# A mixture-of-experts stage on one Trainium2 core: the experts' up weights loaded once into SBUF, and copied slot by slot by ScalarE

## The reference

```python
x = x + attention(_ln_c(x), ...)              # 12 heads, 7x7 neighbourhood, 16 registers
t = _to_tokens(x)
t = t + ffn(_ln_t(t), ...)

# ffn: T = 4608 tokens, 16 experts, top 2, inner width 512; shared expert 1024 wide
scores = jax.nn.softmax(xf @ gate_w.T, axis=-1)
topw, topi = jax.lax.top_k(scores, TOP_K)
comb = jnp.zeros((T, N_EXPERTS), xf.dtype).at[jnp.arange(T)[:, None], topi].set(topw)
h = jax.nn.silu(jnp.einsum('td,eid->tei', xf, w1)) * jnp.einsum('td,eid->tei', xf, w3)
h = h * comb[:, :, None]
y = jnp.einsum('tei,edi->td', h, w2)
z = jax.nn.silu(xf @ sw1.T) * (xf @ sw3.T) @ sw2.T
return (y + z).reshape(Bb, Ss, D)
```

## Time and profile before

| | |
|---|---|
| median of 3 runs | 1109.38 us (1109.3 to 1111.13) |
| profiled execution, its own time | 1112.27 us |
| its span (first to last instruction) | 1110.5 us |
| granted TensorE clock, mean | 0.987 |
| PE busy | 1053.0 us (95%) |
| PEld, DVE, ACT, POOL busy | 855.9, 489.1, 437.7, 486.1 us |
| moved by DMA | 164.39 MB, of which 87 x 768 KB are up weights |

### The profile page before, as it was taken

How to read it: one execution, slowest core, us unless ns; L and a number is a source line. 1 busy time by engine, 2 the same in 40 slices (tenths; PEclk the granted TensorE clock), 3 DMA queues, 4 the chain that set the end, 5 groups by cost and what they waited for, 6 DMA issues and landing times. The chain is left out here.

```text
span 1110.5 us, 32641 instructions
## 1 busy us (share of the span) xinstructions
PE 1053.0 (95%) x12184; PEld 855.9 (77%) x12184; DVE 489.1 (44%) x1826; ACT 437.7 (39%) x974; POOL 486.1 (44%) x746
## 2 busy tenths in 40 slices
PE   6897999999999999899999999999999999999991
PEld 4564777777777766566776777999999999999990
DVE  4664888888888736622222222222222222222220
ACT  2776888888888721111111111222222222222210
POOL 2111556565656400266663000555555555455541
PEclk9998999999999999999999999999999999999996
DMA  4554344444444421023223225888888888788855
GB/s 116 184 196 128 99 133 135 131 138 132 135 134 133 129 57 39 21 60 96 65 66 101 72 69 191 218 221 223 222 223 222 220 222 224 219 224 224 225 132 142
DMA packets 110703, 164.39 MB, mean 148 GB/s; under 512 B 14576, under 2 KB 83848, under 8 KB 110360
## 3 DMA queue, kind: packets, MB, share of 16 engines
q1 hardware_dynamic: 90232, 141.97, 39.6%
q0 software_dynamic: 19056, 20.14, 12.0%
q10 hardware_dynamic: 1264, 0.22, 0.1%
HBM read 130.42 MB, written 35.34 MB: 149 GB/s over the span
## 5 line engine op out<-in xcount | busy, mean ns | idle before, releaser
L627 POOL DMA_INDIRECT acc_dram<-ys,lists x87 | 137.6, 1581 | 255.1 <-DVE ys L1093 152.2
L1086 DVE TENSOR_TENSOR m_h<-m_sg,ps 128x512 f32<-128x512 f32 x87 | 59.8, 688 | 287.2 <-ACT m_sg L748 184.9
L705 ACT ACTIVATE probs<-probs,nmax 128x212 f32<-128x212 f32 x432 | 168.4, 466 | 4.6 <-DVE nmax L858 4.6
L1398 PE MATMUL ps<-xa,w13r 128*128 128x128 f32 x1392 | 169.7, 275 | 0.3 <-ACT xa L742 0.3
L1398 PEld LDWEIGHTS ps<-xa,w13r 128*128 128x128 f32 x1392 | 162.3, 192 | 0.5 <-issue 0.5
L1303 PE MATMUL ps<-c_x,sw13a_sb 64*128 64x384 f32 x768 | 145.6, 489 | 6.3 <-DVE s_h L1041 4.5
L858 DVE CUSTOM_DVE_ANT_0 probs<-ps,bmask 128x212 f32<-128x212 f32 x432 | 134.8, 368 | 24.0 <-PE ps L1209 23.8
L735 ACT ACTIVATE s_sg<-ps 128x384 f32<-128x384 f32 x96 | 47.0, 490 | 240.4 <-PE ps L1303 172.4
L748 ACT ACTIVATE m_sg<-ps 128x512 f32<-128x512 f32 x87 | 51.9, 597 | 219.4 <-PE ps L1403 196.9
L1414 PE MATMUL ps<-w_sb,m_h 128*128 x696 | 136.4, 339 | 0.0
L1223 PE MATMUL ps<-ident_sb,probs 128*98 128x128 f32 x864 | 119.0, 280 | 0.2
(11 more groups left out here) (140 smaller groups left out, 1283.4 us busy)
## 6 DMA issues: line engine op xcount, KB each, us to landing
w13r<-in_w13a SPq DMA_DIRECT2D x87, 512.0 KB
w13r<-in_w13b SPq DMA_DIRECT2D x87, 256.0 KB
vst<-v_dram SPq DMA_DIRECT2D x144, 147.0 KB
v_dram<-a_v SPq DMA_DIRECT2D x12, 576.0 KB, 3.1
w_sb<-in_w SPq DMA_DIRECT2D x8, 768.0 KB
xn_dram<-xn SPq DMA_DIRECT2D x36, 128.0 KB
a_x<-in_x SPq DMA_DIRECT2D x12, 288.0 KB, 3.5
x_p<-in_x SPq DMA_DIRECT2D x36, 96.0 KB
```

Source lines behind the costliest of these rows:

```text
L627: nc.gpsimd.indirect_dma_start(acc_dram, bass.IndirectOffsetOnAxis(ap=lists[:, j, 0:1], axis=0), ys[:, j % V8, :], None, compute_op=ALU.ad ...
L705: nc.scalar.activation(here, here, ACT.Exp, bias=nmax[:, batch % 2, r:r + 1], scale=-1.0).then_inc(b_exp, 1)
L1398: mm(ps[:, g + k, 128 * f:128 * (f + 1)], w13r[:, j % RING, k, 128 * f:128 * (f + 1)], xa[:, j % 2, 0:128], start=f == 0, stop=False, skip ...
```

## The change

The ring of four that SP fills from DRAM is taken away. In its place `w13_sb` holds the up weights of all 16 experts (96 KB per partition). SP loads them in `c_band(0)` to `c_band(7)`, two experts at a time in two transfers (1024 KB and 512 KB), with no wait of their own. In the experts' stage ACT takes the slot's expert number into a register and copies that expert's 1536 columns into a ring of two, `wring`. The copy for slot j waits until up(j-2) is done. ACT's order becomes xT_out(j+1), weights_out(j+1), d_silus(j); the copy for slot 0 waits for the routing, for all 32 weight transfers and for the last up product of the shared expert, whose weights lay where `wring` is. Several tiles get other places in SBUF, among them `s_h`, `s_sg`, `c_x2`, `xg`, `xa` and `w2_sb`; `w13_sb` covers the attention's keys and queries. SP has nothing left to issue between the shared expert and the output.

```diff
-        w13r = place("w13r", [128, RING, 3, INTER], f32, at)
+        w13_sb = place("w13_sb", [128, EX, 3, INTER], f32, at)
...
+        at = [b_end]
+        wring = place("wring", [128, 2, 3, INTER], f32, at)
...
-            def load_w13(j):
-                if j >= RING:
-                    sp.wait_ge(d_a, j - RING + 1)
-                    sp.wait_ge(d_b, j - RING + 1)
-                e = sp.value_load(slot_expert[0:1, j:j + 1], min_val=0, max_val=EX - 1)
-                sp.dma_start(w13r[:, j % RING, 0:2, :], w13a[:, ds(e, 1), :, :].squeeze(1)).then_inc(d_up[j % RING], 16)
-                sp.dma_start(w13r[:, j % RING, 2, :], w13b[:, ds(e, 1), :].squeeze(1)).then_inc(d_up[j % RING], 16)
+            def load_w13(n):
+                two = slice(2 * n, 2 * n + 2)
+                sp.dma_start(w13_sb[:, two, 0:2, :], w13a[:, two, :, :]).then_inc(d_w13, 16)
+                sp.dma_start(w13_sb[:, two, 2, :], w13b[:, two, :]).then_inc(d_w13, 16)
...
-                if n == NB - 1:
-                    for j in range(RING):
-                        load_w13(j)
+                if n < EX // 2:
+                    load_w13(n)
...
-            for j in range(RING, USED):
-                load_w13(j)
...
+            def weights_out(j):
+
+                e = act.value_load(slot_expert[0:1, j:j + 1], min_val=0, max_val=EX - 1)
+                if j >= 2:
+                    act.wait_ge(d_a, j - 1)
+                    act.wait_ge(d_b, j - 1)
+                nc.scalar.copy(wring[:, j % 2, :, :].rearrange("p k x -> p (k x)"),
+                               w13_sb[:].rearrange("p e k x -> p (e k x)")[:, ds(e * (3 * INTER), 3 * INTER)]
+                               ).then_inc(d_wA, 1)
+
+            act.wait_ge(r_done, 1)
+            act.wait_ge(d_w13, 16 * EX)
+            act.wait_ge(c_b, 8 * NB)
+            weights_out(0)
             xT_out(0)
             for j in range(USED):
                 if j + 1 < USED:
                     xT_out(j + 1)
+                    weights_out(j + 1)
                 d_silus(j)
...
-                pe.wait_ge(d_up[j % RING], 32 * (j // RING) + 32)
+                pe.wait_ge(d_wA, j + 1)
```

More of the change, by code:

```diff
@@ L46, in metaformer_block @@
     USED = (2 * T - EX) // 128 + EX
-    RING = 4
     XW = 256
@@ L150, in metaformer_block @@
         at = [arena]
-        w13r = place("w13r", [128, RING, 3, INTER], f32, at)
-        s_h = place("s_h", [128, 8, BAND], f32, at)
-        s_sg = place("s_sg", [128, 2, BAND], f32, at)
+        w13_sb = place("w13_sb", [128, EX, 3, INTER], f32, at)
+        stage = at[0]
+        w2_sb = place("w2_sb", [128, EX, 4, D], f32, at)
+        after_w2 = at[0]
         xg = place("xg", [128, V8, XW], f32, at)
         xa = place("xa", [128, 2, XW], f32, at)
[L156 to L164, removed]
+        assert qk_end <= stage and at[0] <= b_end
         at = [stage]
@@ L182, in metaformer_block @@
         assert at[0] <= after_w2
-        at = [after_w2]
-        c_x2 = place("c_x2", [128, 3, D], f32, at)
-        at = [max(b_end, at[0])]
+        at = [b_end]
         sw13a_sb = place("sw13a_sb", [128, 2, SINTER], f32, at)
@@ L189, in metaformer_block @@
         c_x = place("c_x", [128, 2, 2, BAND], f32, at)
+        s_sg = place("s_sg", [128, 2, BAND], f32, at)
+        c_x2 = place("c_x2", [128, 3, D], f32, at)
+        s_h = place("s_h", [128, 8, BAND], f32, at)
         assert at[0] <= top, at[0]
+        at = [b_end]
+        wring = place("wring", [128, 2, 3, INTER], f32, at)
+        assert at[0] == b_end + 4 * 3 * SINTER
+        at = [at[0] + 4 * 8 * D]
+        m_sg = place("m_sg", [128, 2, INTER], f32, at)
+        m_h = place("m_h", [128, 2, INTER], f32, at)
+        at = [b_end + 4 * (3 * SINTER + 8 * D + 6 * BAND + 3 * D)]
+        ys = place("ys", [128, V8, D], f32, at)
         ps = ctx.enter_context(nc.psum_tensor("ps", [128, 8, 512], f32))
@@ L285, in metaformer_block @@
         d_down = sem("d_down")
-        d_up = sems("d_up", RING)
+        d_w13 = sem("d_w13")
+        d_wA = sem("d_wA")
         d_g = sems("d_g", V8)
@@ L1397, in up @@
                     for k in range(2):
-                        mm(ps[:, g + k, 128 * f:128 * (f + 1)], w13r[:, j % RING, k, 128 * f:128 * (f + 1)],
+                        mm(ps[:, g + k, 128 * f:128 * (f + 1)], wring[:, j % 2, k, 128 * f:128 * (f + 1)],
                            xa[:, j % 2, 0:128], start=f == 0, stop=False, skip_group_check=True)
@@ L1402, in up @@
                         half = slice(64 * k, 64 * (k + 1))
-                        ins = mm(ps[:, g + k, 128 * f:128 * (f + 1)], w13r[half, j % RING, 2, 128 * f:128 * (f + 1)],
+                        ins = mm(ps[:, g + k, 128 * f:128 * (f + 1)], wring[half, j % 2, 2, 128 * f:128 * (f + 1)],
                                  xa[half, j % 2, 128:256], start=False, stop=True, skip_group_check=True)
```

## The result

The changed kernel is faster, by 0.6%. Over 8 runs each, its median is 1105.51 us (1104.32 to 1107.7) against 1112.13 us (1109.3 to 1131.92) of the kernel before, a ratio of 0.9942, 95% interval 0.992 to 0.9965. The forecast was 1107.5 us and most likely no measurable change, by a sum of -1.9 us; -6.6 us were measured between these medians. As much as the median, the spread changed: from 22.6 us between the fastest and the slowest run to 3.4. All ratios here leave out runs more than 1.5% above the fastest of their kernel, while medians and ranges count every run.

What follows compares the result with a forecast made beforehand. The prediction took PE as the bound, at 4.60 us per slot. Removing 3.4 us of backlog, all else 0, gave 1108.9 us from the profiled run or 1106.0 from the median; the middle was 1107.5, range 1105.0 to 1112.5.

Steps and rivals of the forecast that it cites:

- PE untouched: Experts' stage: PE stays at 4.60 us per slot, gaining and losing 0; with a backlog partly or wholly removed, chance 0.55.
- The copy and its place: ACT, each slot: copy 1.53 us plus register load 0.6, together 2.1, fitting the 2.50 us idle before SiLU; cost 0.
- The point from which ACT decides: Experts' stage: cover gone when copy and register load exceed 3.5 us; beyond it each 0.1 us costs 8.6 us.
- Start of the stage and early loads: First expert slots and shared bands 0 to 7: first copies ready in time, added loads fit SP's waits; cost 0.
- rival 3: Shared stage: bursts of the new loads stall PE, up to 8 x 1.84 = 14.7 us, time 1122; chance 0.09.
- the one stalled band: Shared expert: a band with seven gathers beside a down-weight load took 26.0 us against 23.70; 1.84 us lost.
- The backlog: Program's tail: POOL's chain of additions is late through slow landings; without loads the last addition starts 3.4 us earlier.
- The sum: Whole kernel: 1110.5 - 3.4 + 0 = 1107.1 us span, 1108.9 with the 1.77 us around it.
- I take the middle, 1107.5: Forecast median: between 1108.9 us (median run has hardly any backlog) and 1106.0 us (it has it too).
- 3.4 plus 0.1: Program's tail: upper bound of the backlog gain, 3.4 us plus 0.1 for each of two landings, so 3.6.
- Rival 1: Experts' stage: loads were hidden anyway, slow landings having another cause or runs no backlog; time 1109, chance 0.25.
- Rival 4: Whole kernel: all runs carry the backlog and the stalled band goes too, gaining 3.4 + 1.8 us; 1104.2, chance 0.06.

Runs made afterwards that it cites:

- e3: Changed kernel without ACT's copies and register loads, PE reading the resident weights at fixed expert j mod 16 (wrong outputs); ratio 0.9926 to the kernel before, median 1106.9 us.
- e7: Changed kernel with one more ACT copy of 1536 columns per slot, into a spare region; ratio 0.9926 to the kernel before, median 1107.4 us.
- e8: Changed kernel with two more ACT copies of 1536 columns per slot, into spare regions; ratio 1.0164 to the kernel before, median 1134.9 us.
- e1: Kernel before with the up-weight loads of the experts' stage removed and nothing else (wrong weights); ratio 0.9921 to the kernel before, median 1106.6 us.
- e4: Kernel before, unchanged, run and profiled again; ratio 1.0, median 1117.4 us over 12 runs.
- e11: Changed kernel, unchanged, run again; ratio 0.9931 to the kernel before, median 1105.9 us.
- e6: Kernel before with all loads, odd slots' additions going to a second DRAM tensor, each waiting for the addition two before; ratio 0.9887 to the kernel before, median 1104.2 us.
- e9: Changed kernel with each slot's own expert loaded into two unread regions by turns, waiting for the load two before; ratio 1.001 to the kernel before, median 1115.1 us.
- e2: Changed kernel with 512 KB and 256 KB loads per slot put back into one unread region, walking through the experts; ratio 1.0077 to the kernel before, median 1123.9 us.
- e5: Changed kernel with each slot's own expert loaded into one unread region, each load waiting for the last; ratio 1.0495 to the kernel before, median 1172.9 us.
- e10: Kernel before with each up-weight load also waiting for y_mm(j-4), 1.57 us later in the slot; ratio 1.0092 to the kernel before, median 1132.3 us.

## Why the prediction was right, and where its size was off

**PE untouched**: right. The slot takes 4.59 us with 51 or 224 GB/s beside it, and e3 shows that neither copies nor resident weights change that. (The 68 MB of the prediction count all 87 slots; the four loads of band 11 come ahead of the stage, so it is 65 MB.)

**The copy and its place**: right in kind, a little dear. 1.47 us measured for 1.53 (1.50 to 1.82) and 0.33 for the register load of 0.6 (0.3 to 0.8), together 1.8 for 2.1. The point from which ACT decides was put at 3.5 us. e7, with 3.0 us between the end of the x copy and SiLU, costs nothing. e8, with three copies of 1.37, 4.1 us, costs 27. By e8's timeline SiLU and the x copy need 0.76 us before the next copy starts, so the point is near 4.59 - 0.76 = 3.8 us, an estimate. The expectation of e8 was too dear because it added the register load and full copies, which overlap.

**Start of the stage and early loads**: right. The first copy begins at 674.75 us under the down products, and PE's 0.34 us wait for the x copy is 0.33. From one band's first down product to the next, bands 1 to 3 take 26.5, 30.0 and 24.15 us and all later ones 23.68, and this is so with the new loads inside (after) and without them (e1, e4). The bands were not all 23.7 us, as the prediction had them, but the loads add nothing, so rival 3 is refuted; in the prediction it rested on the one stalled band, which e4 shows to be chance.

**The backlog**: the mechanism was right and its 3.4 us measured 3.34 in the two profiles. The row on the Trainium skill (DMA: Bandwidth & Descriptors, Latency and other measured facts) stands as weighed there: an ordinary landing hardly changes without loads (3.6 us with, 3.6 without), so the gain on top that the Trainium skill's row would give did not come. The slowest landings did get shorter by about that much, from 5.6 us to 3.8 in the two profiles. The sign that the prediction gave, every addition 0.84 us behind its rows up to slot 85, holds but for nine slots, 53 to 57 and 68 to 71, which start 0.1 to 1.2 us later than that (slot 36 by 0.06 us).

**The sum**: here the size was off. The step that failed is "I take the middle, 1107.5", and the bound "3.4 plus 0.1" under it. I took the backlog of one execution for its largest value, and three runs at 1109 to 1111 for the usual ones. Later medians of the kernel before are 1112 to 1117, with runs of 1130 to 1147. The chain loses ground by single steps of 5 to 6.4 us and recovers 0.2 to 0.3 us per slot at best, so under load its mean step (4.56 us from slot 56 to 79) is about PE's 4.59. Such a queue has no fixed backlog; it wanders from run to run, and beyond some 11 us it stops PE through the gathers. Taking the loads away was worth 8.0 us on the median in e1, and the whole change 6.6 and 8.8 us (the first comparison and e11), not 1.9; about 1 us of the change's gain (1.4 in the two profiles) may be the earlier start of the shared stage. That the loads cost by the chain is shown by e1, e6 and e9. The runs above 1130 us of the kernel before were not profiled; that they are the same queue further out is argued from e2, e5 and e10, where it was seen. The clock does not make them long: their mean granted clock is 0.981 to 0.983, and runs of 1114 to 1117 us of the same kernel have 0.983 to 0.985. That it is higher, 0.985 to 0.986, in the runs of 1108 to 1111 us fits the backlog: PE idles in the tail and the clock there is granted at 1.2 GHz, for 18.8 us in the profile of the changed kernel, 21.5 in that of the one before and 27.1 in e9.

**Rival 1** (loads hidden anyway), at 0.25 the second likeliest, is refuted by e1 and e9. What it named beside the loads was partly true: the late steps at slots 53 and 68 come without them, and slow landings do occur without them (16 landings over 4.5 us in e3, e7 and e8), all beside packets of the instruction queue, and instruction fetches were its guess. **Rival 4** came nearest in size. That all runs carry a backlog was right; the stalled band, its other half, was chance. The point forecast of 1107.5 us lies 2 us from the measured median, but by luck in part: it counted from three early runs at 1109 us, and the sum's -1.9 us is less than a third of what was measured.

## What to carry to other kernels

Beside the engine that is the bound, look for a serial chain whose mean step is close to that engine's period. It does not show in busy shares, and one profile gives only one value of its backlog; compare the lag at several slots and the spread of the runs. Traffic that is hidden from the bounding engine can still set such a chain's pace, and then when in the cycle it is issued counts as much as how many bytes it moves.

## What the runs showed of the hardware

- The same 768 KB per slot, issued by other waits, make a kernel of 1115 or of 1173 us (e9 and e5). A step of the chain of additions of 128 rows, beside which a load is issued at the addition's start or up to 1.5 us later, takes 5.1 to 6.4 us on average instead of 4.3.
- Packets of the instruction queue go with slow additions: all 16 landings over 4.5 us in profiles without loads had one, 1.5 to 3.5 us behind the addition's start.
- ScalarE instructions that follow one another overlap. In e8 copies recorded at 1.47 us start 1.37 us apart. The register load of each slot (0.28 us on ACT's sequencer) showed 0.33 us of idle time with one copy and none with three.
- Slots 53 and 68 start late in every kernel whose lag was at the floor ahead of them, with loads or without, with one chain or two (e6), by steps of 5.8 and 5.4 us. POOL's idle time there ends by its own issue; why stays open.
